# Lone cross attention of a decoder kernel: two PSUM banks for scores and for transposes, scores one step ahead, output projection in a bank of its own

## What is computed

```
def _L1_xattn_ref(x, context, Wq, Wk, Wv, Wo, bo):
    ...
    q = (x @ Wq).reshape(B, Sq, h, d).transpose(0, 2, 1, 3)
    k = (context @ Wk).reshape(B, -1, h, d).transpose(0, 2, 1, 3)
    v = (context @ Wv).reshape(B, -1, h, d).transpose(0, 2, 1, 3)
    scores = jnp.einsum('bhid,bhjd->bhij', q, k) * scale
    attn = jax.nn.softmax(scores, axis=-1)
    out = jnp.einsum('bhij,bhjd->bhid', attn, v)
    out = out.transpose(0, 2, 1, 3).reshape(B, Sq, h * d)
    return out @ Wo + bo
...
    x = x + _L0_attn_ref(_layernorm(x, axis=-1), ...)
    x = x + _L0_xattn_ref(_layernorm(x, axis=-1), ctx_768, ...)
    x = x + _L0_ffn_ref(_layernorm(x, axis=-1), ...)
    x = x + _L1_attn_ref(_layernorm(x, axis=-1), ...)
    x = x + _L1_xattn_ref(_layernorm(x, axis=-1), ctx_768, ...)
    x = x + _L1_ffn_ref(_layernorm(x, axis=-1), ...)
```

## Time and profile before

| | us |
|---|---|
| median of three runs | 2653.42 (2648.04 to 2653.51) |
| the profiled execution | 2641.24 |
| its span, first to last instruction | 2639.4 |
| PE busy / DVE busy / ACT busy | 2184.3 / 1635.3 / 1029.5 |
| lone cross attention, first scores to last add | 2217.55 to 2329.20 |
| first rows of the experts on PE | 2365.96 |

### The profile page before, as it was taken

One profiled execution on the slowest core, in us unless ns is written; L12 is line 12 of the kernel. 1 busy time (PEld: TensorE's weight loads), 2 busy tenths in 40 slices (PEclk: granted clock), 3 DMA queues, 4 the chain that ended last, 5 costly groups with the idle time before them and its releaser, 6 DMA issues. The chain is left out here.

```text
span 2639.4 us, 31277 instructions
## 1 busy us (share of the span) xinstructions
PE 2184.3 (83%) x11024; PEld 1329.6 (50%) x11024; DVE 1635.3 (62%) x2717; ACT 1029.5 (39%) x1611; POOL 288.8 (11%) x332
## 2 busy tenths in 40 slices
PE   6999999999999988755568887888797879849994
PEld 4666666666666655532223344434443444636663
DVE  5555555555555566546999899979998983220002
ACT  1222222222222222114765776576658742212220
POOL 1111111111111111100100000000000000310005
PEclk8999999999999999877788887979798886559997
DMA  6000100010000000010111111011001101103333
GB/s 218 1 0 17 41 8 0 17 40 9 0 17 25 23 1 0 1 40 33 38 48 39 38 48 38 18 39 48 32 17 54 48 27 60 43 19 100 100 100 111
DMA packets 57469, 102.55 MB, mean 39 GB/s; under 512 B 7828, under 2 KB 39087, under 8 KB 56832
## 3 DMA queue, kind: packets, MB, share of 16 engines
q1 hardware_dynamic: 54272, 93.67, 10.7%
q0 software_dynamic: 3072, 7.28, 0.9%
HBM read 87.10 MB, written 14.94 MB: 39 GB/s over the span
## 5 line engine op out<-in xcount | busy, mean ns | idle before, releaser
L1772 PE MATMUL pa<-arena 128*128 128x512 f32 x512 | 315.5, 747 | 111.9 <-DVE arena L1347 111.9
L1339 DVE TENSOR_TENSOR_SCAN arena<-arena 128x1024 f32<-128x1024 f32 x128 | 292.2, 2283 | 12.3 <-ACT arena L809 12.0
L1550 PE MATMUL pa<-arena 128*128 128x512 f32 x512 | 228.8, 600 | 12.4 <-DVE arena L1011 11.7
L1772 PEld LDWEIGHTS pa<-arena 128*128 128x128 f32 x512 | 106.2, 227 | 248.8 <-DVE arena L1347 146.6
L1560 PE MATMUL po<-arena 128*128 128x256 f32 x1024 | 230.1, 381 | 0.0
L672 ACT COPY arena<-po 128x512 f32<-128x512 f32 x64 | 37.5, 586 | 463.0 <-PE po L1515 463.0
L525 POOL TENSOR_SCALAR arena<-arena 128x2 f32<-128x2 f32 (+1 forms) x92 | 27.5, 299 | 1648.3 <-DVE arena L1206 934.1
L1560 PEld LDWEIGHTS po<-arena 128*128 128x128 f32 x1024 | 191.2, 189 | 31.9 <-issue 3.5
L793 ACT ACTIVATE arena<-arena 128x510 f32<-128x510 f32 x256 | 170.2, 715 | 60.8 <-DVE arena L1339 54.2
L1481 PE MATMUL pt<-arena 128*128 128x128 f32 x756 | 119.8, 289 | 81.9 <-DMA arena<-rows_to_experts 19.9
L1036 DVE TENSOR_TENSOR arena<-pa,arena 128x512 f32<-128x512 f32 x256 | 158.2, 680 | 26.1 <-PE pa L1495 25.3
(11 more groups left out here) (254 smaller groups left out, 3687.2 us busy)
## 6 DMA issues: line engine op xcount, KB each, us to landing
arena<-bc_rows SPq DMA_DIRECT2D x64, 512.0 KB, 4.3
arena<-in_L_ffn_W SPq DMA_DIRECT2D x16, 1024.0 KB, 7.5
arena<-in_L_attn_W SPq DMA_DIRECT2D x8, 1024.0 KB, 5.3
rows_to_experts<-arena SPq DMA_DIRECT2D x4, 1024.0 KB, 12.4
arena<-rows_to_experts SPq DMA_DIRECT2D x8, 512.0 KB, 8.6
rows_from_experts<-arena SPq DMA_DIRECT2D x8, 512.0 KB, 3.3
arena<-in_x SPq DMA_DIRECT2D x4, 512.0 KB, 7.7
arena<-in_rows SPq DMA_DIRECT2D x8, 256.0 KB, 3.2
```

The source lines that it names most:

```text
L1339: v.tensor_tensor_scan(h.rearrange(flat), decay.rearrange(flat), h.rearrange(flat), 0.0, ALU.mult, ALU.add).then_inc(scan_done, 1)
L1550: last = mm(pa[(i + 2) % 4][:, :], w1[:, k, ts(i, P)], yT[:, k, :], start=k == 0, stop=k == KC - 1)
L1772: last = mm(pa[c][:, :], ident, uh[i % len(uh)][:, n, :], start=g == 0 and n == 0, stop=g == NS // NG - 1 and n == NG - 1)
```

## The change

In the lone call alone (`p` and `n` both None) the cross attention uses banks that nothing else needs there: scores alternate between `pt1` and `pt0`, the transposes of the weights between `po0` and `pa3`, and the tile's transposed rows and its output projection share `pa2`. In all other calls the banks and the order stay. With two banks, the scores of step `u + 1` are issued before the transposes of `u`; the copy of `u` on ScalarE moves two slots back, behind the exponentials of `u + 1`; the output projection, and on ScalarE the copy ahead of it and on VectorE the add behind it, move two slots back. Several waits drop out, since the banks that they guarded are no longer shared. The number of instructions is the same.

```
+    lone_score, lone_tr, lone_out = (pt[1], pt[0]), (po[0], pa[3]), pa[2]
+    def cross_banks(p, n):
+        if p is None and n is None:
+            return CrossBanks(True, lone_score, lone_tr, (lone_out, lone_out))
+        return CrossBanks(False, (bank_score, bank_score), (bank_tr, bank_tr), (bank_tr, bank_score))
...
+            at = cross_banks(p, n)
+            drain = 2 if at.lone else 0
...
-                if i % 2 == 1 and 0 <= (i - 3) // 2 < 16:
-                    u = (i - 3) // 2
+                if i % 2 == 1 and 0 <= (i - 3 - drain) // 2 < 16:
+                    u = (i - 3 - drain) // 2
                     act.wait_ge(pT_done, 16 * q + u + 1)
...
-                if i % 8 == 3 and i >= 11:
-                    tile = (i - 11) // 8
+                if i % 8 == 3 + drain and i >= 11 + drain:
+                    tile = (i - 11 - drain) // 8
...
-                    v.tensor_tensor(row_of, bank_score[:, 0:D], row_of, ALU.add).then_inc(wo2_out, 1)
+                    v.tensor_tensor(row_of, at.out[:, 0:D], row_of, ALU.add).then_inc(wo2_out, 1)
...
+            ahead = 1 if at.lone else 0
...
-                if u:
-                    pe.wait_ge(pexp_ready, 16 * q + u)
-                if u >= 6 and u % 4 == 2:
+                if u > ahead:
+                    pe.wait_ge(pexp_ready, 16 * q + u - ahead)
+                if not at.lone and u >= 6 and u % 4 == 2:
                     pe.wait_ge(wo2_out, 4 * q + u // 4)
...
-                if u:
-                    pe.wait_ge(pT_out, 16 * q + u)
-                if u >= 5 and u % 4 == 1:
+                if u > ahead:
+                    pe.wait_ge(pT_out, 16 * q + u - ahead)
+                if not at.lone and u >= 5 and u % 4 == 1:
                     pe.wait_ge(at2T_out, 4 * q + u // 4)
...
-                if i % 2 == 0 and i // 2 < 16:
-                    scores2(i // 2)
+                if at.lone and i == 0:
+                    scores2(0)
+                if i % 2 == 0 and i // 2 + ahead < 16:
+                    scores2(i // 2 + ahead)
...
-                    pe.wait_ge(pT_out, 16 * q + min(4 * tile + 5, 16))
+                    if at.lone:
+                        pe.wait_ge(wo2_out, 4 * q + tile)
+                    else:
+                        pe.wait_ge(pT_out, 16 * q + min(4 * tile + 5, 16))
...
-                if i % 8 == 3 and i >= 11:
+                if i % 8 == 3 + 2 * ahead and i >= 11 + 2 * ahead:
                     tile = i // 8 - 1
                     pe.wait_ge(at2T_out, 4 * q + tile + 1)
-                    pe.wait_ge(pexp_ready, 16 * q + min(4 * tile + 6, 16))
+                    if not at.lone:
+                        pe.wait_ge(pexp_ready, 16 * q + min(4 * tile + 6, 16))
```

More of the change, by code:

```diff
@@ L50 @@
 ACT_STEPS = 2 * UNITS
-CROSS_SLOTS = 36
+CROSS_SLOTS = 38
 ROUTED_EARLY = 43
@@ L174, in begun, with __init__ @@
     return (0, 0, 0) if q is None else (PAIRS, PAIRS, q)
+class CrossBanks:
+    def __init__(self, lone, score, tr, out):
+        self.lone, self.score, self.tr, self.rows, self.out = lone, score, tr, out[0], out[1]
 class Arena:
@@ L827, in cross @@
                         act.wait_ge(av2_done, 16 * q + u - 1)
-                    nc.scalar.copy(pT[u % 2], bank_tr[:, :].rearrange("p (b i) -> p b i", b=4)).then_inc(pT_out, 1)
-                if i % 8 == 3 and i >= 11:
-                    act.wait_ge(at2T_done, 4 * q + (i - 11) // 8 + 1)
-                    nc.scalar.copy(at2T, bank_tr[:, :].rearrange("p (k t) -> p k t", k=QC)).then_inc(at2T_out, 1)
+                    nc.scalar.copy(pT[u % 2], at.tr[u % 2][:, :].rearrange("p (b i) -> p b i", b=4)).then_inc(pT_out, 1)
+                if i % 8 == 3 + drain and i >= 11:
+                    act.wait_ge(at2T_done, 4 * q + (i - 11 - drain) // 8 + 1)
+                    nc.scalar.copy(at2T, at.rows[:, :].rearrange("p (k t) -> p k t", k=QC)).then_inc(at2T_out, 1)
             if p is not None:
@@ L1305, in cross @@
                     dve.wait_ge(s2_done, 16 * q + u + 1)
-                    step.after(v.tensor_reduce(mx[:, u % 4, :], bank_score[:, :].rearrange("p (b j) -> p b j", b=2), AX, ALU.max))
+                    step.after(v.tensor_reduce(mx[:, u % 4, :], at.score[u % 2][:, :].rearrange("p (b j) -> p b j", b=2), AX, ALU.max))
                     v.tensor_scalar(nm[:, u % 4, :], mx[:, u % 4, :], -SCALE, None, ALU.mult).then_inc(nm_ready, 1)
@@ L1794, in weights_transposed @@
                     for k in range(2):
-                        last = transposed(bank_tr[:, ts(2 * b + k, P)], pexp[u % 2][:, b, ts(k, P)])
+                        last = transposed(at.tr[u % 2][:, ts(2 * b + k, P)], pexp[u % 2][:, b, ts(k, P)])
                 last.then_inc(pT_done, 1)
@@ L1850, in cross @@
                     pe.wait_ge(at2_ready, 4 * q + tile + 1)
-                    pe.wait_ge(pT_out, 16 * q + min(4 * tile + 5, 16))
+                    if at.lone:
+                        pe.wait_ge(wo2_out, 4 * q + tile)
+                    else:
+                        pe.wait_ge(pT_out, 16 * q + min(4 * tile + 5, 16))
                     for c in range(QC):
-                        last = transposed(bank_tr[:, ts(c, P)], at2[:, ts(c, P)])
+                        last = transposed(at.rows[:, ts(c, P)], at2[:, ts(c, P)])
                     last.then_inc(at2T_done, 1)
-                if i % 8 == 3 and i >= 11:
+                if i % 8 == 3 + 2 * ahead and i >= 11 + 2 * ahead:
                     tile = i // 8 - 1
                     pe.wait_ge(at2T_out, 4 * q + tile + 1)
-                    pe.wait_ge(pexp_ready, 16 * q + min(4 * tile + 6, 16))
+                    if not at.lone:
+                        pe.wait_ge(pexp_ready, 16 * q + min(4 * tile + 6, 16))
                     for c in range(QC):
-                        last = mm(bank_score[:, 0:D], at2T[:, c, :], w_o[:, c, :], start=c == 0, stop=c == QC - 1)
+                        last = mm(at.out[:, 0:D], at2T[:, c, :], w_o[:, c, :], start=c == 0, stop=c == QC - 1)
                     last.then_inc(wo2_done, 1)
@@ L1895, in mixer @@
             if q is not None:
-                cross(UNITS + 3)
+                for i in range(UNITS + 3, UNITS + 4 + 2 * ahead):
+                    cross(i)
             if n is not None:
```

7 lines of the change are left out of this document (4 added, 3 removed).

## The result

| | before | after |
|---|---|---|
| median of the runs timed side by side | 2651.18 (18 runs, 2647.75 to 2653.78) | 2657.16 (18 runs, 2651.68 to 2660.74) |
| ratio, 95% interval | | 1.002 (1.0013 to 1.0027) |
| the profiled execution | 2641.24 | 2657.16 |
| its span | 2639.4 | 2655.4 |
| first scores to last add | 111.65 | 122.24 |

The changed kernel is 6 us slower (0.1 to 0.3%), where 3.4 us faster was forecast. In the two profiles the stretch is 10.6 us longer; 2.6 lie ahead of it and 2.8 behind it, in code that is the same.

A forecast was written before the change was run, and what follows sets the result against it. TensorE at its lower clock was taken to bound the 111.65 us stretch: 114.3 us with waits traded, less 6.0 for full clock, gives 108.3, so -3.4 us and 2650.0 from 2653.4. Range 2641 to 2659.

The forecast's parts named there:

- TensorE's own work and the waits: First scores to last add: 95.2 us of TensorE work in both kernels; 15.0 us of waits go, 16.1 come.
- The four large waits that came: Weighted sum waiting for ScalarE's copy: 3.3, 2.9 and 3.1 us beside routing, 3.1 behind the third projection.
- the scalings: In two turns reciprocal and scaling alone stand ahead of the maxima on VectorE: 0.65 us each, 1.3 in all.
- the adds: A projection's add now stands ahead of the maxima on VectorE: 1.1 us of new wait, twice.
- the old turns: Three turns where exponentials stood behind the rows' copy and scores awaited projection and add: 2.5 us each, 7.6 go.
- the ordinary steps: Transposes start 2.11 us after the weighted sum where 1.76 is possible: 0.35 in eight steps, 2.9 us go.
- The waits are traded, not removed: At one and the same clock, 16.1 us of waits come and 15.0 go in the stretch: +1.1 us.
- six stretches of full clock: TensorE's clock rises in six stretches instead of one, each saving 1.0 to 1.1 us net: -6.0 us.
- At most turns: Longer unbroken TensorE runs should raise its clock at most turns between tiles; it would fall again in the waits.
- already at the transposed rows: At the turns, TensorE's clock perhaps rises as early as the transposes of the tile's rows.
- I carry the difference over: Whole kernel: the runs' median lies 12 us above the profiled execution; kept unchanged, so 2653.4 - 3.4 = 2650.0.
- Slower by over 5.3 us: Whole kernel slower by more than 5.3 us, through satisfied waits costing like open ones or the clock staying down: 0.17.

The follow-up runs named there:

- e17: The changed kernel, unedited, on a chip where the kernel before took 2641.44 us: 2641.34 us, 1.0003 of before.
- e1: The changed kernel with ScalarE's copy put back ahead of the next exponentials: 2636.88 us, 0.9949 of before.
- e5: The changed kernel with the copy back ahead of the exponentials and the first 24 scatters spread, two a step: 2610.15 us, 0.9877 of before.
- e7: The changed kernel with the first 24 scatters spread, two a step: 2645.81 us, 1.0007 of before.
- e4: The changed kernel, unedited, profiled once more: 2653.12 us (1 run), stretch 122.22 us.
- e14: The changed kernel with the first 24 scatters spread, two a step, on another chip: 2641.82 us, 1.0002 of before.
- e3: The kernel before, unedited, profiled once more: 2648.97 us (1 run), stretch 118.31 us.
- e11: The kernel before, unedited, on a further chip: 2660.35 us (1 run), stretch 122.36 us.
- e12: The changed kernel, unedited, on a further chip: 2654.18 us (1 run), stretch 122.15 us.
- e16: The changed kernel with the first 24 scatters moved behind the stretch, so none runs beside the cross attention: 2662.08 us (1 run), stretch 109.69 us.
- e10: The changed kernel with the copy back ahead of the exponentials and scatters spread two a step, on a further chip: 2613.48 us, 0.9858 of before.
- e15: The changed kernel with the copy back ahead of the exponentials and scatters spread four a step: 2612.26 us, 0.9886 of before.
- e9: The changed kernel with the copy back ahead of the exponentials, scatters in a row, on a further chip: 2635.88 us, stretch 101.92 us.
- e8: The changed kernel with the first 24 scatters moved behind the stretch, behind the last pair's deviations: 2657.36 us (1 run), stretch 102.02 us.

## Why the prediction was wrong

**TensorE's own work and the waits: right.** Without late events the sum can be tested. It had 114.3 us at the lower clock and 18.9 us of waits with the tail, to which the profile adds the 2.02 that it counts ahead of the first transposes though the second scores run in it: 20.9 against 21.49 in e17 (of which 0.28 lie ahead of the first scores). The four large waits that came are within 0.4 us each; at the scalings 0.50 us came for 0.65, at the adds, at full clock, 1.7 to 1.8 for 1.1. Those of the old turns and of the ordinary steps are gone. "The waits are traded, not removed" stands. e1 shows by which part: the copy behind the next exponentials. The prediction costed it (9.3 us beside the routing, 3.1 behind the third projection) but saw it only as part of a package. Its cost is 114.3 - 100.7 = 13.6 us by the arithmetic at the lower clock; without it the stretch is 33 us shorter (e5 against e7), and the clock is up for 30.7 us in e5 where it is up three times for 3.4 in e7.

**The clock: right in kind, wrong in number.** Forecast were six stretches of full clock at 1.0 us net. There were three, in all of e4, e7, e14 and e17: 114.3 - 3 x 1.05 = 111.1 by the prediction's own price of 1.0 to 1.1 for each, and e17 has 111.13. "At most turns" was right, three of four; the step that failed is "I take six such stretches instead of one", which counted on a rise "already at the transposed rows" too. It rose only behind projections, and in e17 a wait of 1.69, 1.79 or 2.85 us stood right there each time, so that TensorE was busy for 1.72, 1.62 and 0.56 us of 3.41 (in after for 0.94, 2.03 and 1.00, windows above). Worth of the change, like for like: 111.13 - 111.65 = -0.5 us instead of -3.4. That is e17 against the kernel before: 1.0003.

Whether transposes count for the clock is not settled by this: here it rose behind projections, which are no transposes, and e5 held it up for 30.7 us in steps where transposes take 0.54 of 2.54 us. The rule of the Trainium skill (TensorE: Matmul & The Clock Gate, Part 4), that they do not count, is neither borne out nor refuted by these rows.

**The baseline: wrong, and this is the larger part.** The step was "the median of the runs shown is 12 us above the profiled one; I carry the difference over". It took an unexplained 12 us for a constant that the change leaves alone, and so put at nothing what the new order would make of its cause. On chips A and C most of it is TensorE's late events beside the scatter: 6.7 and 10.7 us in the stretch of the kernel before (118.31 and 122.36 against 111.65), 11.0 to 11.1 in that of the changed kernel, three times (122.24, 122.22, 122.15 against 111.13). The first profile of before showed none, as on chips B, D and E; the timed runs of the kernel before lay at 2651, as on A and C, and the profile of after has late events.

In the stretches seen the new order does not wait longer for late events. TensorE's waits in the stretch grew by 15.1 and 12.7 us in the kernel before (29.21 in e3 and 26.85 in e11, against 14.14) and by 10.9 to 11.2 in the changed one (32.71 in after, 32.49 in e4, 32.41 in e12, against 21.49). But the kernel before got part of it back by the clock, above all in e3 (windows there), and the new order did not: its clock rose three times for 3.4 us with late events or without.

So of the 6 us, -0.5 is the change's own, and late events cost the new order 0.3 to 4.4 us more in the stretches seen. The rest, 2 to 6 us, is not accounted for: e4 is 4.2 us above e3, and e12 below e11, which began its stretch 5.8 us later than e12 did. One look each does not tell the two kernels' mean cost of late events.

**Chances.** "Slower by over 5.3 us" had 0.17, by a mechanism that did not occur, and the range ended at 2659, so that it held 2657.2; that it did is luck. No rival said that an event could come late. The rows ahead of the prediction could not show it either; the gap of 12 us was the only sign.

**What stays open.** Why TensorE's events come late beside a row of scatters on some chips and not on others; each chip was used in one sitting, so whether it is the chip or its state at the time is not told apart. The nine traces with late events also hold fewer records of the engines' semaphore updates, 5330 to 5336 where each of the other ten has 5355; whether the recording has a part in the delays is not ruled out by these runs. Whether a scatter is needed for it: e16 found no chip that could tell. Spread scatters were tested on such a chip only in the reordered kernel (e10), not in the kernels before and after, and the reordered kernel without spread scatters was not run on a chip free of late events, so that its gain there is inferred from e5 and e15, whose scatters are spread, those of e15 hardly. Where the rest of the 6 us comes from.

## What to carry to other kernels

When scores are issued one step ahead, let the copy of this step's transposes stay ahead of the next exponentials on ScalarE: the second bank already frees TensorE, and a copy placed behind them ties the weighted sum to all that VectorE does before the next maxima. Both together (two banks, scores ahead, copy first, scatters spread) took 30 to 37 us off, 1.1 to 1.4% (e5, e10, e15): 13.6 by the arithmetic of the waits, the rest as TensorE ran nearly without gaps and kept its clock (28.46 of 30.72 us busy at full clock in e5); on the chips with late events the spread scatters have their part in it too. Where the timed runs lie well above the profiled one, profile again, on another chip if there is one, before anything is built on that profile.

## What the runs showed of the hardware

- Two kinds of chip, as each was seen in one sitting. The same kernel before takes 2641.4 to 2643.3 us on three and 2649.7 to 2650.0 on two (medians of 7 to 19 runs). On the slower two, each of the seven traces of a kernel whose scatters stood in a row has late TensorE events beside them; on the others none of the nine traces read has any, though only e17 among them has its scatters in a row.
- A TensorE event can reach ScalarE or VectorE long after the matmuls ended: the add of e9 began at 2276.14, 14 us behind the end of its projection (2258.33 and 3.62). With the 24 scatters spread over 50 us in place of 31 the latest was 1.8 us late (e10). ScalarE's and VectorE's own events were never over 0.02 us late.
- The same happens at another place of the slower chips, far from the change. POOL gathers 16 tiles in a row from 2594.15 on (L640), and an add of the experts (L1479 on VectorE) then waits 26.64 us, for an event marked "remote", where it waited 21.97 in e17. It is so in e3, e9 and e10 too, in e10 with its first scatters spread, since the gathers are not. Here it costs nothing: the add after it starts 29.49 us behind the one before it, in after (2589.74 and 2619.23) as in e17 (2574.98 and 2604.47). From there to the end it is 36.1 us in after, but 34.9 in e17 and 34.9 in e3, which has the late event as well. Timeline of after and, behind it, of e17:

```profile
2617.07 0.69 DVE L1479 TENSOR_TENSOR arena<-po,arena 128x512 f32<-128x512 f32 x1 [26.64 <-remote]
2619.23 0.69 DVE L1479 TENSOR_TENSOR arena<-po,arena 128x512 f32<-128x512 f32 x1 [1.47 <-PE po L2015]
```

```profile
2597.64 0.69 DVE L1479 TENSOR_TENSOR arena<-po,arena 128x512 f32<-128x512 f32 x1 [21.97 <-PE po L2015]
2604.47 0.69 DVE L1479 TENSOR_TENSOR arena<-po,arena 128x512 f32<-128x512 f32 x1 [6.14 <-PE po L2015]
```

- The clock can go either way in one and the same program. e8 and e16 are the same kernel, without late events; in e8 the clock stayed up for 20.5 us of the stretch at one time, in e16 it came up three times for 3.4. The stretches are 102.02 and 109.69. Window of e8 and, at nearly the same time, of e16:

```profile
2294.07:2314.55 20.48, 13.91 (x83) 10.62 (x81) 5.57 (x14) 7.54 (x26) 0.00 (x0) 1.00 0.00 1
```

```profile
2294.50:2315.00 20.50, 18.46 (x70) 14.31 (x70) 4.26 (x11) 6.48 (x21) 0.00 (x0) 0.58 0.00 1
```
